# Layer-0 routed experts on one Trainium2 core: the turn of the Gelu products placed behind the next block's gate and up products, down products two steps behind

## The chip, the core and the metric

The kernel runs on one NeuronCore of a Trainium2 chip. The metric is the device time of one execution in microseconds (us). A core has TensorE (PE; its weight loads are PEld in the profile), VectorE (DVE), ScalarE (ACT), GpSimd (POOL) and the queue engine SP; they run their own instruction streams and wait for each other by semaphores.

## What is computed

Two transformer layers over x of 2048 rows of 512 float32. Each is attention, layer norm, mixture of experts, layer norm. The change touches the routed experts of layer 0; cut to that part the reference is

```python
def _experts_all(x, g, gb, w1, b1, w2, b2):       # gelu is the exact one
    y = jax.nn.gelu(jnp.einsum('bsd,edf->bsef', x, g) + gb, approximate=False)
    y = y * (jnp.einsum('bsd,edf->bsef', x, w1) + b1)
    return jnp.einsum('bsef,efd->bsed', y, w2) + b2

aff = jax.nn.sigmoid(jnp.einsum('bsd,de->bse', x, wa))
topk_p, topk_i = jax.lax.top_k(aff, K)            # K = 2 of E = 16 experts
topk_p = topk_p / jnp.sum(topk_p, axis=-1, keepdims=True)
combine = jnp.sum(jax.nn.one_hot(topk_i, E, dtype=x.dtype) * topk_p[..., None], axis=2)
routed = jnp.einsum('bsed,bse->bsd', _experts_all(x, rg, rgb, rw1, rb1, rw2, rb2), combine)
```

with d = 512 and f = 256. Only the two chosen experts of a row are computed by the kernel.

## The kernel before, in words

`two_layers` runs its stages one after the other: `attention0`, `experts0_shared` (which also makes the routing tables), `experts0_routed`, `attention1` (which gathers the experts' results), `experts1_shared`, `experts1_routed`, `combine1`. Between stages all engines meet.

Matmuls in float32 precision are made of three: every operand is split into a high part (a copy to fp32r, made by ScalarE) and a low part (original minus high, made by VectorE), and `mm3` (lines 66 to 68) issues high x high, high x low and low x high.

`experts0_routed` works on NG0 = 47 blocks of 128 gathered rows, numbered g. The routing sorts the rows by expert into groups of 128. Block g = 4h + p takes group 12p + h, so that four columns (p = 0 to 3) walk through the groups side by side; blocks that share p share raw buffers, so raw buffers are four deep. The split tiles (`w1_hi`, `w2_lo`, `xt_hi`, `hf`, ...) and the PSUM banks are two deep (g % 2). For each block:

- GpSimd asks for three indirect DMAs: `rows` (L1043, 256 KB of token rows into `xg`), `gate_up` (L1051, 1 MB of gate and up weights into `w1_raw`) and `down` (L1059, 512 KB of down weights into `w2_raw`). `load_of` holds an index out of bounds where the group before in the column has the same expert; nothing is moved then. Each request for a block waits until the block four earlier has let its buffer go: `rows` for the turn of the tokens, `gate_up` for the low split L1176, `down` for the low split L1193.
- TensorE: `turn` (L1082, four transposes of the tokens), `gate_up` (12 matmuls of 512 columns and the bias L1097), `turn_hidden` (L1104, two transposes of the Gelu products `hf`), `down` (six matmuls of 512 columns).
- ScalarE: `turned_hi` (L1128, high part of the turned tokens), `hidden_hi` (L1142, high part of the turned products), `weights_hi` (L1135, 128 x 2048), the copy of the down weights (L1149, 128 x 1024) and Gelu (L1153), both in `gelu`, and `results` (L1160, the output to `y`, which SP stores).
- VectorE: `turned_lo` (L1180), `hidden_lo` (L1184), `weights_lo` (L1176, 128 x 2048), and in `hidden` the product `hf` = Gelu x up (L1191), followed by the low part of the down weights (L1193, 128 x 1024).

The order is written out by hand. A step g of TensorE is `turn`(g+1), `turn_hidden`(g-1), `gate_up`(g), `down`(g-1). `three_stages` gives a step of ScalarE as turned_hi(g+1), hidden_hi(g-1), weights_hi(g+1), gelu(g), results(g-1), and of VectorE as turned_lo(g+1), hidden_lo(g-1), weights_lo(g+1), hidden(g). TensorE and GpSimd are written out in full; ScalarE and VectorE run a loop of four steps a round.

Of the kernel before, what the change touches and what calls it, by code (L numbers as in the profile page):

```python
# [487 lines left out]
def three_stages(eng, n, first, second, third, ahead=no_work, between=no_work, prepare=no_work, unroll=2, lead=3):  # L488

    def step(g):

        for stage, item in ((ahead, g + lead), (first, g + 1), (between, g - 1), (prepare, g + 1), (second, g), (third, g - 1)):
            if 0 <= item < n:
                stage(item // unroll, item % unroll)


    rounds = (n - lead - 1) // unroll
    for g in range(-lead, unroll + 1):
        step(g)
    with eng.Fori(1, rounds) as i:
        for q in range(unroll):
            at = lambda stage, item: stage(i + item // unroll, item % unroll)
            at(ahead, q + lead + 1)
            at(first, q + 2)
            at(between, q)
            at(prepare, q + 2)  # L510
            at(second, q + 1)
            at(third, q)
    for g in range(unroll * rounds + 1, n + 1):
        step(g)


# [7 lines left out]
NG0 = (2 * T) // GRP + E0 - 1  # L524
# [465 lines left out]
def experts0_routed(k):  # L990
# [3 lines left out]
    U = U0  # L994
    with ExitStack() as ctx:
# [22 lines left out]
        nothing = lambda h, p: None  # L1018
# [3 lines left out]
        with nc.Block() as block:  # L1022
# [52 lines left out]
            @block.tensor  # L1075
            def _(pe):
                def turn(h, p):
                    pe.wait_ge(s_g[p], 16 * (h + 1))
                    if past(h, p, 2):
                        pe.wait_ge(s_tlo, U * h + p - 1)  # L1080
                    for b in range(KD):
                        mm = pe.transpose(bank[p % 2][:, b * P:(b + 1) * P], xg[p][:, b * P:(b + 1) * P], k.ident[:, :])  # L1082
                    mm.then_inc(s_tps, 1)

                def gate_up(h, p):
                    g = U * h + p
                    if not past(h, p, 1):
                        pe.wait_ge(s_b1lo, 1)
                    pe.wait_ge(s_wlo, g + 1)
                    pe.wait_ge(s_tlo, g + 1)  # L1090
                    if past(h, p, 2):
                        pe.wait_ge(s_h, g - 1)
                    out = bank[2 + p % 2][:, :]
                    for b in range(KD):
                        t, c = slice(b * P, (b + 1) * P), slice(b * 2 * F0, (b + 1) * 2 * F0)
                        mm3(pe, out, xt_hi[p][:, t], xt_lo[p][:, t], w1_hi[p][:, c], w1_lo[p][:, c], b == 0, False)
                    pe.matmul(out, k.expert_here[:, NH0 * p + h:NH0 * p + h + 1].to_broadcast([P, P]), b1[:, :], start=False, stop=True).then_inc(s_gu, 1)  # L1097

                def turn_hidden(h, p):
                    pe.wait_ge(s_h, U * h + p + 1)  # L1100
                    if past(h, p, 2):
                        pe.wait_ge(s_hlo, U * h + p - 1)
                    for f in range(FB):
                        mm = pe.transpose(bank[4 + p % 2][:, f * P:(f + 1) * P], hf[p][:, f * P:(f + 1) * P], k.ident[:, :])  # L1104
                    mm.then_inc(s_ht, 1)

                def down(h, p):
                    g = U * h + p
                    pe.wait_ge(s_hlo, g + 1)
                    pe.wait_ge(s_vlo, g + 1)  # L1110
                    if past(h, p, 2):
                        pe.wait_ge(s_ysb, g - 1)
                    for f in range(FB):
                        t, c = slice(f * P, (f + 1) * P), slice(f * D, (f + 1) * D)
                        mm = mm3(pe, bank[6 + p % 2][:, :], ht_hi[p][:, t], ht_lo[p][:, t], w2_hi[p][:, c], w2_lo[p][:, c],
                                 f == 0, f == FB - 1)
                    mm.then_inc(s_dn, 1)

                for g in range(-1, NG0 + 1):
                    for stage, item in ((turn, g + 1), (turn_hidden, g - 1), (gate_up, g), (down, g - 1)):  # L1120
                        if 0 <= item < NG0:
                            stage(item // U, item % U)

            @block.scalar
            def _(act):
                def turned_hi(h, p):
                    act.wait_ge(s_tps, U * h + p + 1)
                    act.activation(xt_hi[p][:, :], bank[p % 2][:, :], ACT.Copy).then_inc(s_thi, 1)  # L1128

                def weights_hi(h, p):  # L1130
                    g = U * h + p
                    act.wait_ge(s_w[p], 16 * (h + 1))
                    if past(h, p, 2):
                        act.wait_ge(s_gu, g - 1)
                    act.activation(w1_hi[p][:, :], w1_raw[p][:, :], ACT.Copy).then_inc(s_whi, 1)  # L1135

                def hidden_hi(h, p):
                    g = U * h + p
                    act.wait_ge(s_ht, g + 1)
                    if past(h, p, 2):  # L1140
                        act.wait_ge(s_dn, g - 1)
                    act.activation(ht_hi[p][:, :], bank[4 + p % 2][:, 0:FB * P], ACT.Copy).then_inc(s_hh, 1)  # L1142

                def gelu(h, p):
                    g = U * h + p
                    act.wait_ge(s_v[p], 16 * (h + 1))
                    if past(h, p, 2):
                        act.wait_ge(s_dn, g - 1)
                    act.activation(w2_hi[p][:, :], w2_raw[p][:, :], ACT.Copy).then_inc(s_vhi, 1)  # L1149
                    act.wait_ge(s_gu, g + 1)  # L1150
                    if past(h, p, 2):
                        act.wait_ge(s_h, g - 1)
                    act.activation(ge[p][:, :], bank[2 + p % 2][:, 0:F0], ACT.Gelu).then_inc(s_ge, 1)  # L1153

                def results(h, p):
                    g = U * h + p
                    act.wait_ge(s_dn, g + 1)
                    if past(h, p, U):
                        act.wait_ge(s_y[p], 16 * h)
                    act.activation(y[p][:, :], bank[6 + p % 2][:, :], ACT.Copy).then_inc(s_ysb, 1)  # L1160

                three_stages(act, NG0, turned_hi, gelu, results, between=hidden_hi, prepare=weights_hi, unroll=U)

            @block.vector
            def _(vec):
                lo_rows = slice(32, 32 + E0)
                vec.wait_ge(s_b1, 32)
                vec.wait_ge(s_zero, 1)
                vec.tensor_copy(b1[0:E0, :], b1_raw[0:E0, :]).then_inc(s_b1hi, 1)
                vec.tensor_copy(b1_hi[lo_rows, :], b1_raw[lo_rows, :]).then_inc(s_b1hi, 1)  # L1170
                vec.wait_ge(s_b1hi, 2)
                vec.tensor_tensor(b1[lo_rows, :], b1_raw[lo_rows, :], b1_hi[lo_rows, :], ALU.subtract).then_inc(s_b1lo, 1)

                def weights_lo(h, p):
                    vec.wait_ge(s_whi, U * h + p + 1)
                    vec.tensor_tensor(w1_lo[p][:, :], w1_raw[p][:, :], w1_hi[p][:, :], ALU.subtract).then_inc(s_wlo, 1)  # L1176

                def turned_lo(h, p):
                    vec.wait_ge(s_thi, U * h + p + 1)
                    vec.tensor_tensor(xt_lo[p][:, :], bank[p % 2][:, :], xt_hi[p][:, :], ALU.subtract).then_inc(s_tlo, 1)  # L1180

                def hidden_lo(h, p):
                    vec.wait_ge(s_hh, U * h + p + 1)
                    vec.tensor_tensor(ht_lo[p][:, :], bank[4 + p % 2][:, 0:FB * P], ht_hi[p][:, :], ALU.subtract).then_inc(s_hlo, 1)  # L1184

                def hidden(h, p):
                    g = U * h + p
                    vec.wait_ge(s_ge, g + 1)
                    if past(h, p, 2):
                        vec.wait_ge(s_ht, g - 1)  # L1190
                    vec.tensor_tensor(hf[p][:, :], ge[p][:, :], bank[2 + p % 2][:, F0:2 * F0], ALU.mult).then_inc(s_h, 1)  # L1191
                    vec.wait_ge(s_vhi, g + 1)
                    vec.tensor_tensor(w2_lo[p][:, :], w2_raw[p][:, :], w2_hi[p][:, :], ALU.subtract).then_inc(s_vlo, 1)  # L1193

                three_stages(vec, NG0, turned_lo, hidden, nothing, between=hidden_lo, prepare=weights_lo, unroll=U)


H1, DH1, FM = 16, 32, 64
# [1495 lines left out]
```

## Time and profile before

| | us |
|---|---|
| median of 3 runs (1604.08 to 1609.27) | 1608.56 |
| the profiled execution, its own time | 1606.87 |
| its span in the trace | 1605.1 |
| first token transpose of the stage | at 428.33 |
| last copy of its results | at 693.10 |

Times in the trace count from the start of the span. A row of the timeline gives start, duration, engine, line, what is written and read, and in brackets how long the engine stood idle before and who ended that. A row of the waits gives who waited for whom, total, number of times and longest. A request on GpSimd is a DMA_INDIRECT; its own duration is the engine's, the transfer lands later.

### The profile page before, as it was taken

To read this page: it belongs to the slowest core of one execution; us is meant where nothing else is said; L and a number is where in the kernel's file an instruction comes from. 1 tells how busy PE (TensorE), PEld (TensorE's weight loads), DVE (VectorE), ACT (ScalarE), POOL (GpSimd) and SP (SyncE) were. 2 spreads that over 40 slices of the span, in tenths; PEclk is the share of its full clock that TensorE was granted. 3 is DMA by queue.
4 is the path that set the end of the run, shared out by engine and by line. 5 is a ranking of instruction groups with operands and counts; after the bars stand their busy time and mean duration, and the time that the engine had idled before them with its cause. 6 is when DMAs were issued, how large, how long until landed. Compare 5 with 4: busy or idle time off the path is not lost. (4 is left out here: it accounts for less than half of the span.)

```text
span 1605.1 us, 21477 instructions
## 1 busy us (share of the span) xinstructions
PE 1358.1 (85%) x7252; PEld 1118.4 (70%) x7253; DVE 1074.1 (67%) x1792; ACT 728.6 (45%) x1157; POOL 750.3 (47%) x656
## 2 busy tenths in 40 slices
PE   6999869999699999925999689996698899999960
PEld 5787647766477777725999688995566777777740
DVE  5688747232388888846885556764393688888857
ACT  4121132000188888822554354441422388888850
POOL 1455510000488887632664324331056467777744
PEclk9899979999799999967999899997799799999995
DMA  4000040000456566533110100000512899999958
GB/s 165 1 1 27 27 132 2 1 0 0 161 190 222 170 208 226 171 120 95 52 53 2 31 3 1 28 27 27 194 40 103 319 335 341 342 346 346 345 134 314
DMA packets 81807, 212.67 MB, mean 132 GB/s; under 512 B 20425, under 2 KB 23497, under 8 KB 79291
## 3 DMA queue, kind: packets, MB, share of 16 engines
q1 hardware_dynamic: 50075, 133.14, 22.7%
q0 software_dynamic: 31120, 77.38, 17.0%
q8 instruction: 51, 0.84, 0.2%
q10 hardware_dynamic: 528, 1.05, 0.2%
q14 instruction: 33, 0.27, 0.1%
HBM read 208.75 MB, written 46.79 MB: 159 GB/s over the span
## 5 line engine op out<-in xcount | busy, mean ns | idle before, releaser
L66 PE MATMUL bank<-e_w_hi,e_xt_hi 128*96 128x384 f32 (+1 forms) x444 | 169.3, 381 | 3.4 <-DVE e_w_lo L2551 3.4
L68 PE MATMUL bank<-e_w_hi,e_xt_lo 128*96 128x384 f32 (+1 forms) x444 | 161.8, 364 | 0.0
L67 PE MATMUL bank<-e_w_lo,e_xt_hi 128*96 128x384 f32 (+1 forms) x444 | 161.3, 363 | 0.0
L1051 POOL DMA_INDIRECT e_w_raw<-in_w_gate_up,r_load_of x47 | 53.4, 1135 | 218.5 <-issue 218.5
L2441 POOL DMA_INDIRECT sums<-e_y,r_target_of x64 | 110.2, 1722 | 70.1 <-DMA sums<-e_y,r_target_of 44.0
L1176 DVE TENSOR_TENSOR e_w_lo<-e_w_raw,e_w_hi 128x2048 fp32r<-128x2048 f32 x47 | 107.7, 2292 | 33.8 <-ACT e_w_hi L1135 33.8
L2551 DVE TENSOR_TENSOR e_w_lo<-r_w_early,e_w_hi 128x1536 fp32r<-128x1536 f32 x48 | 84.9, 1768 | 24.4 <-ACT e_w_hi L2515 24.4
L1043 POOL DMA_INDIRECT e_xg<-rows,r_token_of x47 | 93.2, 1983 | 14.3 <-issue 14.3
L231 POOL TENSOR_TENSOR a_read<-a_read_n 128x256 f32<-128x256 f32 x64 | 50.2, 785 | 103.1 <-DVE a_read_n L452 103.1
L1675 POOL TENSOR_TENSOR q_g_lo<-q_gf,q_g_hi 128x512 fp32r<-128x512 f32 x32 | 41.5, 1298 | 111.9 <-ACT q_g_hi L1789 111.9
L1135 ACT ACTIVATE e_w_hi<-e_w_raw 128x2048 fp32r<-128x2048 f32 x47 | 89.8, 1910 | 0.0
L66 PE MATMUL bank<-e_w_hi,e_ht_hi 128*96 128x512 f32 (+1 forms) x222 | 87.6, 395 | 2.4 <-DVE e_ht_lo L2563 1.2
L67 PE MATMUL bank<-e_w_lo,e_ht_hi 128*96 128x512 f32 (+1 forms) x222 | 87.4, 394 | 0.0
L68 PE MATMUL bank<-e_w_hi,e_ht_lo 128*96 128x512 f32 (+1 forms) x222 | 87.1, 392 | 0.0
L66 PEld LDWEIGHTS bank<-e_w_hi,e_xt_hi 128*96 128x96 f32 (+1 forms) x444 | 77.6, 175 | 12.3 <-DVE e_w_lo L2551 3.6
L68 PEld LDWEIGHTS bank<-e_w_hi,e_xt_lo 128*96 128x96 f32 (+1 forms) x444 | 77.6, 175 | 11.9
L67 PEld LDWEIGHTS bank<-e_w_lo,e_xt_hi 128*96 128x96 f32 (+1 forms) x444 | 78.0, 176 | 8.8
L66 PE MATMUL bank<-s_xt_hi,s_w_hi 128*128 128x512 f32 (+1 forms) x192 | 77.0, 401 | 0.8 <-ACT s_scores L2200 0.8
L68 PE MATMUL bank<-s_xt_hi,s_w_lo 128*128 128x512 f32 (+1 forms) x192 | 76.1, 396 | 0.0
L67 PE MATMUL bank<-s_xt_lo,s_w_hi 128*128 128x512 f32 (+1 forms) x192 | 75.7, 394 | 0.0
L2515 ACT ACTIVATE e_w_hi<-r_w_early 128x1536 fp32r<-128x1536 f32 x48 | 71.3, 1484 | 0.0
L1059 POOL DMA_INDIRECT e_w_raw<-in_w_down,r_load_of x47 | 60.5, 1287 | 17.3 <-issue 16.1
(461 smaller groups left out, 4361.7 us busy)
## 6 DMA issues: line engine op xcount, KB each, us to landing
r_w_early<-in_w_gate_up SPq DMA_DIRECT2D x48, 768.0 KB, 16.6
r_w_early<-in_w_down SPq DMA_DIRECT2D x24, 768.0 KB, 13.2
results<-e_y SPq DMA_DIRECT2D x47, 256.0 KB, 5.0
rows<-resid SPq DMA_DIRECT2D x8, 1024.0 KB, 4.3
r_w_first<-in_w_gate_up SPq DMA_DIRECT2D x8, 768.0 KB, 16.4
e_w_raw<-in_w_down SPq DMA_DIRECT2D x8, 768.0 KB, 13.5
e_w_raw<-in_w_gate_up SPq DMA_DIRECT2D x8, 768.0 KB, 16.1
resid<-in_x SPq DMA_DIRECT2D x4, 1024.0 KB, 12.5
```

What stands on the lines that cost most here:

```text
L66: pe.matmul(out, a_hi, b_hi, start=start, stop=False)
L67: pe.matmul(out, a_hi, b_lo, start=False, stop=False)
L68: return pe.matmul(out, a_lo, b_hi, start=False, stop=stop)
L231: pool.tensor_tensor(read_2[:, v % 2, :], read_n[:, v % 2, 0:256], read_n[:, v % 2, 256:512], ALU.add).then_inc(s_r2, 1)
L1043: pool.indirect_dma_start(xg[p][:, :], None, k.rows, bass.IndirectOffsetOnAxis(k.token_of[:, c:c + 1], 0)).then_inc(s_g[p], 16)
L1051: pool.indirect_dma_start(w1_raw[p][:, :], None, io["w_gate_up0"], bass.IndirectOffsetOnAxis(k.load_of[:, c:c + 1], 0), bounds_check=E0 * ...
L1059: pool.indirect_dma_start(w2_raw[p][:, :], None, io["w_down0"], bass.IndirectOffsetOnAxis(k.load_of[:, c:c + 1], 0), bounds_check=E0 * P - ...
L1135: act.activation(w1_hi[p][:, :], w1_raw[p][:, :], ACT.Copy).then_inc(s_whi, 1)
L1176: vec.tensor_tensor(w1_lo[p][:, :], w1_raw[p][:, :], w1_hi[p][:, :], ALU.subtract).then_inc(s_wlo, 1)
L2441: pool.indirect_dma_start(k.sums[p % 2], bass.IndirectOffsetOnAxis(k.target_of[:, e:e + 1], 0), y[p][:, :], None, compute_op=ALU.add).then ...
L2515: act.activation(w1_hi[p][:, :, :], w1_raw[p][:, :, :], ACT.Copy).then_inc(s_whi, 1)
L2551: vec.tensor_tensor(w1_lo[p][:, :, :], w1_raw[p][:, :, :], w1_hi[p][:, :, :], ALU.subtract).then_inc(s_wlo, 1)
```

## The change

`turn_hidden` moves behind `gate_up` on TensorE, and `down` goes from one step behind to two. ScalarE and VectorE follow: the down weights' two splits leave `gelu` and `hidden`, become `down_hi` and `down_lo`, and stand one step later, behind the parts of the turned products. A new helper `pipeline` takes the stages of an engine with how far each is ahead and issues them in that order. Buffers, GpSimd's queue, SP's stores and every single instruction stay as they are.

```diff
+def pipeline(eng, n, unroll, *stages):
+
+    def step(g):
+        for stage, ahead in stages:
+            if 0 <= g + ahead < n:
+                stage((g + ahead) // unroll, (g + ahead) % unroll)
+
+    first, last = -max(ahead for _, ahead in stages), -min(ahead for _, ahead in stages)
+    rounds = (n + first - 1) // unroll
+    for g in range(first, 2 * unroll + 1):
+        step(g)
+    with eng.Fori(2, rounds) as i:
+        for q in range(unroll):
+            for stage, ahead in stages:
+                stage(i + (q + 1 + ahead) // unroll, (q + 1 + ahead) % unroll)
+    for g in range(unroll * rounds + 1, n + last):
+        step(g)
...
-                for g in range(-1, NG0 + 1):
-                    for stage, item in ((turn, g + 1), (turn_hidden, g - 1), (gate_up, g), (down, g - 1)):
+                for g in range(-1, NG0 + 2):
+                    for stage, item in ((turn, g + 1), (gate_up, g), (turn_hidden, g - 1), (down, g - 2)):
...
-                def gelu(h, p):
+                def down_hi(h, p):
                     g = U * h + p
                     act.wait_ge(s_v[p], 16 * (h + 1))
                     if past(h, p, 2):
                         act.wait_ge(s_dn, g - 1)
                     act.activation(w2_hi[p][:, :], w2_raw[p][:, :], ACT.Copy).then_inc(s_vhi, 1)
+
+                def gelu(h, p):
+                    g = U * h + p
                     act.wait_ge(s_gu, g + 1)
...
-                three_stages(act, NG0, turned_hi, gelu, results, between=hidden_hi, prepare=weights_hi, unroll=U)
+                pipeline(act, NG0, U, (turned_hi, 1), (weights_hi, 1), (gelu, 0), (hidden_hi, -1), (down_hi, -1), (results, -2))
...
-                    vec.wait_ge(s_vhi, g + 1)
+
+                def down_lo(h, p):
+                    vec.wait_ge(s_vhi, U * h + p + 1)
                     vec.tensor_tensor(w2_lo[p][:, :], w2_raw[p][:, :], w2_hi[p][:, :], ALU.subtract).then_inc(s_vlo, 1)
...
-                three_stages(vec, NG0, turned_lo, hidden, nothing, between=hidden_lo, prepare=weights_lo, unroll=U)
+                pipeline(vec, NG0, U, (turned_lo, 1), (weights_lo, 1), (hidden, 0), (hidden_lo, -1), (down_lo, -1))
```

TensorE before, from the bias matmul that ends one block's gate and up to the first matmul of the next block's:

```order
L1097 MATMUL bank<-e_b,r_expert_here 128x512
L66 MATMUL bank<-e_w_hi,e_ht_hi 128x512
L67 MATMUL bank<-e_w_lo,e_ht_hi 128x512
L68 MATMUL bank<-e_w_hi,e_ht_lo 128x512
L66 MATMUL bank<-e_w_hi,e_ht_hi 128x512
L67 MATMUL bank<-e_w_lo,e_ht_hi 128x512
L68 MATMUL bank<-e_w_hi,e_ht_lo 128x512
L1082 MATMUL bank<-ident,e_xg 128x128 x4
L1104 MATMUL bank<-ident,e_hf 128x128 x2
L66 MATMUL bank<-e_w_hi,e_xt_hi 128x512
```

and the same place with the change (L1101 is L1082 before, L1116 is L1097, L1123 is L1104):

```order
L1116 MATMUL bank<-e_b,r_expert_here 128x512
L1123 MATMUL bank<-ident,e_hf 128x128 x2
L66 MATMUL bank<-e_w_hi,e_ht_hi 128x512
L67 MATMUL bank<-e_w_lo,e_ht_hi 128x512
L68 MATMUL bank<-e_w_hi,e_ht_lo 128x512
L66 MATMUL bank<-e_w_hi,e_ht_hi 128x512
L67 MATMUL bank<-e_w_lo,e_ht_hi 128x512
L68 MATMUL bank<-e_w_hi,e_ht_lo 128x512
L1101 MATMUL bank<-ident,e_xg 128x128 x4
L66 MATMUL bank<-e_w_hi,e_xt_hi 128x512
```

The two transposes of the products (L1104, L1123) moved from between the token transposes and gate and up to between gate and up and down.

VectorE before, one step (numbers are the buffers; `w1_raw3` is block 3):

```order
L1180 TENSOR_TENSOR e0_xt_lo1<-bank1,e0_xt_hi1 128x512
L1184 TENSOR_TENSOR e0_ht_lo1<-bank5,e0_ht_hi1 128x256
L1176 TENSOR_TENSOR e0_w1_lo1<-e0_w1_raw3,e0_w1_hi1 128x2048
L1191 TENSOR_TENSOR e0_hf0<-e0_ge0,bank2 128x256
L1193 TENSOR_TENSOR e0_w2_lo0<-e0_w2_raw2,e0_w2_hi0 128x1024
```

and with the change (L1202 is L1180 before, L1198 is L1176, L1213 is L1191, L1206 is L1184, L1217 is L1193):

```order
L1202 TENSOR_TENSOR e0_xt_lo1<-bank1,e0_xt_hi1 128x512
L1198 TENSOR_TENSOR e0_w1_lo1<-e0_w1_raw3,e0_w1_hi1 128x2048
L1213 TENSOR_TENSOR e0_hf0<-e0_ge0,bank2 128x256
L1206 TENSOR_TENSOR e0_ht_lo1<-bank5,e0_ht_hi1 128x256
L1217 TENSOR_TENSOR e0_w2_lo1<-e0_w2_raw1,e0_w2_hi1 128x1024
```

The low part of the turned products moved from ahead of the gate and up split to behind the product, and the down split in a step is that of block 1 where it was that of block 2.

## Rows read from the trace of the kernel before

**Rows 1.** The page: span, and part 1, busy time of each engine

```profile
span 1605.1 us, 21477 instructions
...
PE 1358.1 (85%) x7252; PEld 1118.4 (70%) x7253; DVE 1074.1 (67%) x1792; ACT 728.6 (45%) x1157; POOL 750.3 (47%) x656
```

**Rows 2.** Timeline, VectorE: gate and up split of blocks 2 and 46

```profile
445.23 2.29 DVE L1176 TENSOR_TENSOR e_w_lo<-e_w_raw,e_w_hi 128x2048 fp32r<-128x2048 f32 x1 [0.69 <-ACT e_w_hi L1135]
...
682.49 2.29 DVE L1176 TENSOR_TENSOR e_w_lo<-e_w_raw,e_w_hi 128x2048 fp32r<-128x2048 f32 x1 [0.69 <-ACT e_w_hi L1135]
```

**Rows 3.** Waits, 440 to 700 us: total, times, longest

```profile
DVE e_w_lo L1176 <- ACT e_w_hi L1135: 32.7, 46, 1.1
...
PEld bank L1104 <- DVE e_hf L1191: 18.4, 46, 1.0
```

**Rows 4.** Timeline, 565.8 to 571.5 us, one step on TensorE, ScalarE and VectorE

```profile
565.86 0.60 PE L1082 MATMUL bank<-ident,e_xg 128*128 128x128 f32 x4
...
566.11 0.41 DVE L1191 TENSOR_TENSOR e_hf<-e_ge,bank 128x256 f32<-128x256 f32 x1
566.44 1.22 DVE L1193 TENSOR_TENSOR e_w_lo<-e_w_raw,e_w_hi 128x1024 fp32r<-128x1024 f32 x1
566.55 0.59 ACT L1128 ACTIVATE e_xt_hi<-bank 128x512 fp32r<-128x512 f32 x1
566.58 0.44 PE L1104 MATMUL bank<-ident,e_hf 128*128 128x128 f32 x2
...
566.77 0.47 PE L66 MATMUL bank<-e_w_hi,e_xt_hi 128*128 128x512 f32 x1
...
567.05 0.39 ACT L1142 ACTIVATE e_ht_hi<-bank 128x256 fp32r<-128x256 f32 x1
...
567.33 1.91 ACT L1135 ACTIVATE e_w_hi<-e_w_raw 128x2048 fp32r<-128x2048 f32 x1
...
569.27 2.29 DVE L1176 TENSOR_TENSOR e_w_lo<-e_w_raw,e_w_hi 128x2048 fp32r<-128x2048 f32 x1 [0.69 <-ACT e_w_hi L1135]
...
569.60 0.40 PE L1097 MATMUL bank<-e_b,r_expert_here 128*128 128x512 f32 x1
...
571.21 0.60 PE L1082 MATMUL bank<-ident,e_xg 128*128 128x128 f32 x4
...
571.49 0.41 DVE L1191 TENSOR_TENSOR e_hf<-e_ge,bank 128x256 f32<-128x256 f32 x1
```

**Rows 5.** Timeline, the same step on GpSimd, its three requests

```profile
567.33 1.19 POOL L1051 DMA_INDIRECT e_w_raw<-in_w_gate_up,r_load_of  x1 [0.31 <-issue]
568.83 0.99 POOL L1059 DMA_INDIRECT e_w_raw<-in_w_down,r_load_of  x1 [0.30 <-issue]
570.12 2.29 POOL L1043 DMA_INDIRECT e_xg<-rows,r_token_of  x1 [0.30 <-issue]
```

**Rows 6.** Timeline, 431 to 436 us, GpSimd and VectorE while the stage fills

```profile
431.75 0.96 POOL L1043 DMA_INDIRECT e_xg<-rows,r_token_of  x1 [0.30 <-issue]
431.91 2.29 DVE L1176 TENSOR_TENSOR e_w_lo<-e_w_raw,e_w_hi 128x2048 fp32r<-128x2048 f32 x1 [1.11 <-ACT e_w_hi L1135]
433.02 2.04 POOL L1059 DMA_INDIRECT e_w_raw<-in_w_down,r_load_of  x1 [0.31 <-issue]
```

**Rows 7.** DMA issues, us to landing: 460 to 500 us; 497 to 498.5 us

```profile
e_w_raw<-in_w_gate_up,r_load_of POOLq DMA_INDIRECT x8, 3.4
...
e_xg<-rows,r_token_of POOLq DMA_INDIRECT x8, 5.4
...
e_w_raw<-in_w_gate_up,r_load_of POOLq DMA_INDIRECT x1, 7.6
```

**Rows 8.** Timeline, 441 to 443 us: token transposes and their copy, ScalarE free

```profile
441.44 0.60 PE L1082 MATMUL bank<-ident,e_xg 128*128 128x128 f32 x4
...
442.08 0.60 ACT L1128 ACTIVATE e_xt_hi<-bank 128x512 fp32r<-128x512 f32 x1
```

## The prediction

> **What bounds the kernel now.** The page comes first: the profiled execution spans 1605.1 us, TensorE is its busiest engine [rows 1]. The change touches only layer 0's routed experts: 47 blocks of 128 rows, some 260 us. I count in steps, one block a step. From the split of block 2's gate and up weights to that of block 46 there are 44 steps in 682.49 - 445.23 = 237.26 us, **5.39 us a step** [rows 2].
>
> The waits of the stage come next [rows 3]. TensorE's weight loads stood before the turn of the Gelu products (L1104) 46 times, 18.4 us in all: 0.40 us a step, what the change aims at. Just as steady is VectorE's wait for ScalarE before L1176, 32.7 us.
>
> One step in order of time says why [rows 4]. Take T = 565.86, the first transpose of the next block's tokens. The product `hf` begins at T+0.25, because VectorE was at L1176; the turn L1104 follows at 566.58, ScalarE copies it out at 567.05, and only then takes the next block's weights (567.33). L1176 waits for that until 569.27, and the next product comes 2.22 us later (the gap between the products of two steps is again 5.38). So the step is a ring: product, turn (0.47), copy (0.47), weight copy (0.28), L1176 (1.94), product (2.22), 5.38 in sum. TensorE waits since the ring is longer than its own work: its matmuls follow at 0.230 us (seven in 571.21 - 569.60 = 1.61).
>
> The last view is GpSimd's queue, which asks for every load of the stage [rows 5, 6]. Undisturbed, a request takes 0.96 us [rows 6], and the next begins 0.30 later. Requests that meet a VectorE instruction with two SBUF inputs end 0.85 us after that instruction. In rows 6 the one from 433.02 meets L1176, which ends at 434.20, and ends itself at 435.06. In rows 5 the one from 567.33 meets the down split L1193 (ends 567.66) and ends at 568.52; the one from 570.12 meets L1176 (ends 571.56) and ends at 572.41. One that begins 0.16 us before L1176 goes through (431.75, 0.96 us). So a request needs something at about 0.13 us after its start that VectorE holds, then 0.85 more. Per step GpSimd makes three requests: one is released by L1176's end, one by the down split's end, and the third needs a gap of 0.85 + 0.30 + 0.13 = 1.28 us after the latter, before L1176 begins again.
>
> **The change part by part.** No instruction is added or removed. What moves:
>
> 1. TensorE: the turn of the products goes behind gate and up, down products to the next step. The ring is broken. Without waits TensorE needs 19 x 0.230 = 4.37, six transposes at about 0.11 (0.19 to 0.23 for two, from 566.58 to the next matmul, estimated 0.64 in all) = 5.01, and one loop jump of ScalarE and VectorE in four steps, about 0.02 to 0.05 a step: **5.06**. Bounds: 4.99, if the whole 0.40 [rows 3] goes, and 5.11, if only the 0.28 between four transposes' 0.44 and the 0.72 from 565.86 to 566.58 goes. Gain alone: 0.33 x 44 = 14.5 us.
>
> 2. ScalarE: weight copy right behind the token copy, at T+0.69+0.49 = T+1.18 rather than T+1.47. VectorE's L1176 then runs from T+3.12 to T+5.41. Gate and up of that block are to begin at T+5.06+0.44 = T+5.50: 0.1 in hand, so this costs nothing, but a later load shows at once.
>
> 3. VectorE: the order is now L1176, product, low part of the turned products (0.33), **down split**. The down split ends 2.22+0.33+0.33+1.22 = 4.10 us after L1176's start; before, 2.22+0.33+1.22 = 3.77. That changes GpSimd's sum. It gets its third request in a step only if the step is at least 3.77+1.28 = 5.05 before (it was 5.39) and 4.10+1.28 = **5.38** after. A 5.06 step is too short by 0.32: GpSimd then makes two requests of three and falls behind, until TensorE waits for loads.
>
> 4. The down request of a block waits for the down split four blocks earlier, which comes a step later. The row request and the gate-and-up request of the next block are queued behind it. Their lead shrinks: before, the gate-and-up request at T+1.47 was ten us ahead of its use (two steps), the row request likewise, so landing times of 5.4 and 7.6 us [rows 7] were hidden.
>
> 5. What is late next. Once GpSimd is behind, a block's row request is released by the down split's end; the rows land about 3.9 us after release (5.4 from start less the 1.44 us held: rows 5, 7); turn, token copy and weight copy take 0.64 [rows 8] +0.49+1.94 = 3.07 to the next L1176. This loop spans two steps: (4.10+3.9+3.07)/2 = **5.53 us a step** where no new weights are loaded, 0.14 worse than before.
>
> 6. Steps with new weights. `load_of` skips a load when the block before in its column has the same expert. The reference's own routing of its inputs gives 19 real loads in 47 blocks, 15 of them behind the first four: 5, 6, 13, 14, 16, 21, 22, 26, 30, 32, 33, 36, 37, 41, 42. A skipped load is through in 3.4 us, a real one takes 7.6 [rows 7]. In the loop of point 5 the gate-and-up request begins 1.15 after the rows' release and its copy on ScalarE is due at 3.9+1.13 = 5.03, so 3.9 us later: a skipped load just fits, a real one is 3.7 late. Some 0.5 of it is in hand before gate and up. The step is then 8.3 or so, 2.9 over before.
>
> I carried these terms block by block through the stage as a recurrence (each instruction starts when its engine is free and its inputs are there). With the old order it gives 5.39 a step and row landings of 5.4, 7.1 and 8.2 us, which is a check. With the new order: seven steps with a first load +2.9 each = 20.3; two where GpSimd had caught up, +0.9 = 1.8; six second loads in a row +1.1 = 6.6 (rows queue behind 1.5 MB of weights); nine steps behind a load -0.28 = -2.5, since a stall lets GpSimd catch up; the 20 plain ones +0.14 = 2.8. Sum **+29**. Filling is 2.3 shorter (no down products in the first step), draining 2.1 longer (one more step with the last down split before it); together nothing. Later stages start later by the same amount. 1606.87 + 29 = **1636 us**. The profiled execution lies 0.1% under the median of 1608.56, within the spread of its three runs.
>
> The Trainium skill (SBUF — State Buffer, Who interferes with whom) says that a VectorE tensor_tensor never has a two-port mode and did not stall a GpSimd-issued DMA in its probe, with only GpSimd's reads held by two SBUF inputs. The rows above show such requests held, 2.04 and 2.29 us against 0.96; these are indirect ones, so reading the index could be what is held. By the probe's outcome points 3 and 5 would fall away.
>
> **The rivals.**
> - *Faster: GpSimd keeps its lead.* If requests can slip into the gaps or a request's need comes earlier than 0.13, no load is late and only point 1 stays: 1606.87 - 14 = 1593. It decides at a step of 5.38; for it speaks that before the change no TensorE wait for a load is left once the stage runs. Against it: 0.32 us missing is twice what rows 6 leave open. 0.14.
> - *VectorE does not hold requests at all* (rows 5 and 6 would be chance). Then only point 4 is left: real loads 1 to 2 us late, -14 + 15 x 1 to 1.5 = between -6 and +9: 1607. Chance 0.07.
> - *Only the pace is lost, loads stay hidden.* Stalls give back enough lead: 44 x 0.14 = +6, 1613. Chance 0.12.
> - *Worse:* a request slips a slot in every plain step, the loop is (4.10+1.28+3.9+3.07)/2 = 6.18, or the TensorE clock drops to its lower level in the stalls: 44 x 0.79 = 35 plus a third of the loads' sum, some 1655. Chance 0.07.
> - The forecast: 0.60.
>
> **How the numbers follow.** A measurement tells about 0.3% (4.8 us) from no change. Faster: 0.14 and a bit of the second rival, 0.16. Same: most of the second and a little of the third, 0.09. Slower: 0.75. The recurrence moves between +22 and +43 when landing and load times are varied within the rows. The range of 1606 to 1652 leaves out the fast case and half of the worst.
>
> **What the profile after would show.** Right: weight-load waits for the products (L1104, now L1123) gone; new waits of TensorE on `e_xg`'s DMA in plain steps and of ScalarE on `e_w_raw`'s DMA in blocks 5, 13, 16, 21; GpSimd requests of over 2 us twice a step instead of once; steps of 5.5 and 8 us side by side; some 29 us more in the stage. Wrong: an even step near 5.06 with no DMA release before TensorE, or request durations that don't end 0.85 us after a VectorE split.

## The result and the profile after

| | us | before on the same chips | ratio |
|---|---|---|---|
| changed kernel, median of 4 runs | 1643.17 (1636.09 to 1646.78) | 1606.38 (1604.08 to 1609.27) | 1.0227 (1.0204 to 1.025) |
| predicted | 1636.0 (1606 to 1652) | 1608.56 | |
| profiled execution | 1636.09 | 1606.87 | |

It is slower, by 37 us at the medians. The profiled execution was the fastest of the four; the three without a profile took 1640.74 to 1646.78. So the trace below accounts for some 30 us, and another 5 to 11 us of the other runs have no trace of their own.

The page of the changed kernel, with the span and part 1, answers to [rows 1]:

```profile
span 1634.4 us, 21478 instructions
...
PE 1366.7 (84%) x7253; PEld 1123.9 (69%) x7253; DVE 1074.5 (66%) x1792; ACT 732.9 (45%) x1157; POOL 764.5 (47%) x656
```

No engine was given more work, but GpSimd, which only asks for transfers in this stage, is busy 14.2 us longer, and TensorE 8.6 us. Of the latter 7.6 lie in the stage: the same 1175 matmuls take 257.98 rather than 250.37 us, at a granted clock of 0.95 on average rather than 0.98. The timeline of the changed kernel, with the first token transpose and the last copy of results of the stage (start, duration, engine, instruction, idle before it and what ended it):

```profile
425.58 1.11 PE L1101 MATMUL bank<-ident,e_xg 128*128 128x128 f32 x4 [8.44 <-DMA e_xg<-rows,r_token_of]
...
720.19 0.60 ACT L1182 ACTIVATE e_y<-bank 128x512 f32<-128x512 f32 x1 [1.22 <-PE bank L68]
```

The stage takes 294.6 us; between the same two instructions of before it was 693.10 - 428.33 = 264.8. Filling and draining are nearly even (29.8 in the stage, 44 x 0.66 = 29.1 in the steps). All of the difference of the two spans (29.3) is in this stage (29.8). The splits of blocks 2 and 46, VectorE's timeline of the changed kernel, answer to [rows 2]:

```profile
441.77 2.29 DVE L1198 TENSOR_TENSOR e_w_lo<-e_w_raw,e_w_hi 128x2048 fp32r<-128x2048 f32 x1 [1.11 <-ACT e_w_hi L1154]
...
708.10 2.29 DVE L1198 TENSOR_TENSOR e_w_lo<-e_w_raw,e_w_hi 128x2048 fp32r<-128x2048 f32 x1 [2.26 <-ACT e_w_hi L1154]
```

44 steps in 266.33 us, **6.05 us a step** instead of 5.39. The waits of the changed kernel, 430 to 730 us (total, times, longest), answer to [rows 3]:

```profile
DVE e_w_lo L1198 <- ACT e_w_hi L1154: 60.3, 43, 5.8
PEld bank L1101 <- DMA e_xg<-rows,r_token_of: 36.9, 26, 6.8
...
ACT e_w_hi L1154 <- DMA e_w_raw<-in_w_gate_up,r_load_of: 31.6, 16, 5.1
...
POOL e_w_raw L1078 <- DVE e_w_lo L1217: 25.5, 10, 6.8
...
PEld bank L66 <- DVE e_w_lo L1198: 12.4, 15, 2.2
```

The wait that the change aims at (the turn of the products, now L1123, on `e_hf`) is not in the list any more; it was 18.4 us. In its place stand two waits for transfers: the tokens' transposes for the gathered rows, 26 times, and ScalarE for the gate and up weights, 16 times. VectorE's 60.3 is the same lateness seen one engine on, and is not to be added.

Why transfers are late is read from VectorE and GpSimd side by side. Timeline of the changed kernel, 476 to 488 us, blocks without a real load:

```profile
476.65 2.29 DVE L1198 TENSOR_TENSOR e_w_lo<-e_w_raw,e_w_hi 128x2048 fp32r<-128x2048 f32 x1 [0.87 <-ACT e_w_hi L1154]
...
477.61 2.20 POOL L1078 DMA_INDIRECT e_w_raw<-in_w_down,r_load_of  x1 [0.30 <-issue]
...
479.53 1.22 DVE L1217 TENSOR_TENSOR e_w_lo<-e_w_raw,e_w_hi 128x1024 fp32r<-128x1024 f32 x1
...
480.11 1.47 POOL L1062 DMA_INDIRECT e_xg<-rows,r_token_of  x1 [0.30 <-issue]
...
481.88 0.99 POOL L1070 DMA_INDIRECT e_w_raw<-in_w_gate_up,r_load_of  x1 [0.30 <-issue]
...
487.63 2.29 DVE L1198 TENSOR_TENSOR e_w_lo<-e_w_raw,e_w_hi 128x2048 fp32r<-128x2048 f32 x1 [0.41 <-ACT e_w_hi L1154]
...
487.76 3.02 POOL L1070 DMA_INDIRECT e_w_raw<-in_w_gate_up,r_load_of  x1 [0.30 <-issue]
```

The down request ends at 479.81, 0.87 after L1198's end (478.94); the row request at 481.58, 0.83 after the down split's end (480.75). The third finds the gap and takes 0.99. That is the forecast's picture, with two held requests a step. The last pair is a missed slot: the request begins 0.13 us after L1198 and is held for all of it, 3.02 us; in [rows 6] one that began 0.16 before L1176 went through. The fence also shows what does not happen: L1198 takes 2.29 us whether or not a request meets it.

A step behind a real load (block 13), same view, 507 to 510 us:

```profile
507.05 1.91 ACT L1154 ACTIVATE e_w_hi<-e_w_raw 128x2048 fp32r<-128x2048 f32 x1 [3.23 <-DMA e_w_raw<-in_w_gate_up,r_load_of]
...
509.00 2.29 DVE L1198 TENSOR_TENSOR e_w_lo<-e_w_raw,e_w_hi 128x2048 fp32r<-128x2048 f32 x1 [3.43 <-ACT e_w_hi L1154]
...
509.61 0.66 PE L1101 MATMUL bank<-ident,e_xg 128*128 128x128 f32 x4 [1.53 <-DMA e_xg<-rows,r_token_of]
```

ScalarE waits 3.23 us for the weights, VectorE 3.43 for ScalarE; this step takes 8.13 us.

The durations of all 47 row requests (lowest/median/highest in ns, first to last us, by line), the changed kernel first, then before:

```profile
L1062 POOL DMA_INDIRECT e_xg<-rows,r_token_of x47: 960/1466/2982, 420.7 to 699.5; - x47
```

```profile
L1043 POOL DMA_INDIRECT e_xg<-rows,r_token_of x47: 962/2286/2737, 423.3 to 669.8; - x47
```

Before, the row request alone paid for L1176 in most steps, and the step had room for it. After, row, gate-and-up and down requests take turns in paying, and some pay 3.0 us. Of the 141 requests of all three kinds, 80 take over 1.2 us instead of 47.

### The profile page after: what moved, and what is told of

Its sections match the earlier page's. It is cut to its first block and busy times, and to the rows that moved or that the text cites. A ratio compares the mean times of both kernels' runs of the same rounds, so it can differ in the third digit from the quotient of the medians.

```text
span 1634.4 us, 21478 instructions
## 1 busy us (share of the span) xinstructions
PE 1366.7 (84%) x7253; PEld 1123.9 (69%) x7253; DVE 1074.5 (66%) x1792; ACT 732.9 (45%) x1157; POOL 764.5 (47%) x656
## 5 line engine op out<-in xcount | busy, mean ns | idle before, releaser
L66 PE MATMUL bank<-e_w_hi,e_xt_hi 128*96 128x384 f32 (+1 forms) x444 | 172.6, 389 | 12.2 <-DVE e_w_lo L1198 8.7
L1070 POOL DMA_INDIRECT e_w_raw<-in_w_gate_up,r_load_of x47 | 69.4, 1476 | 215.6 <-issue 215.6
L1198 DVE TENSOR_TENSOR e_w_lo<-e_w_raw,e_w_hi 128x2048 fp32r<-128x2048 f32 x47 | 107.8, 2293 | 60.3 <-ACT e_w_hi L1154 60.3
L1078 POOL DMA_INDIRECT e_w_raw<-in_w_down,r_load_of x47 | 81.9, 1743 | 37.5 <-DVE e_w_lo L1217 25.5
L66 PE MATMUL bank<-e_w_hi,e_ht_hi 128*96 128x512 f32 (+1 forms) x222 | 91.9, 414 | 2.6 <-issue 1.4
L1062 POOL DMA_INDIRECT e_xg<-rows,r_token_of x47 | 69.4, 1476 | 14.3 <-issue 14.3
```

What stands on the lines that cost most here:

```text
L66: pe.matmul(out, a_hi, b_hi, start=start, stop=False)
L1062: pool.indirect_dma_start(xg[p][:, :], None, k.rows, bass.IndirectOffsetOnAxis(k.token_of[:, c:c + 1], 0)).then_inc(s_g[p], 16)
L1070: pool.indirect_dma_start(w1_raw[p][:, :], None, io["w_gate_up0"], bass.IndirectOffsetOnAxis(k.load_of[:, c:c + 1], 0), bounds_check=E0 * ...
L1078: pool.indirect_dma_start(w2_raw[p][:, :], None, io["w_down0"], bass.IndirectOffsetOnAxis(k.load_of[:, c:c + 1], 0), bounds_check=E0 * P - ...
```

## The experiments

Theory A is the forecast's: two-input VectorE instructions hold GpSimd's requests, the down split now stands too late for three requests a step (point 3), and a down request waiting for its buffer keeps the next rows and weights behind it (point 4). Its rivals: holding is harmless and only the queue order counts; only real loads are late and the pace does not matter; the new order itself costs TensorE time. (The letters B to F in the recorded expectations stand for what each of them says beside its letter.) "Stage" below is from the first token transpose to the last copy of results.

| kernel | us | before | ratio (interval) | stage us | us a step |
|---|---|---|---|---|---|
| before | 1606.38 | | | 264.8 | 5.39 |
| after | 1643.17 | 1606.38 | 1.0227 (1.0204 to 1.025) | 294.6 | 6.05 |
| e1 no real loads | 1624.18 | 1605.0 | 1.0113 (1.0095 to 1.013) | 283.7 | 5.82 |
| e2 before, no real loads | 1605.29 | 1605.0 | 1.000 (0.9989 to 1.001) | 263.9 | 5.39 |
| e3 one SBUF input | 1607.99 | 1605.0 | 1.0019 (1.0 to 1.0038) | 267.8 | 5.46 |
| e4 one input, no real loads | 1597.13 | 1605.0 | 0.9942 (0.9925 to 0.9958) | 255.8 | 5.18 |
| e5 down request later | 1622.9 | 1604.23 | 1.0118 (1.0096 to 1.0141) | 282.6 | 5.79 |
| e6 one input, request later | 1599.06 | 1604.23 | 0.9973 (0.9963 to 0.9983) | 259.6 | 5.23 |
| e7 down split earlier | 1626.51 | 1604.25 | 1.0139 (1.0108 to 1.017) | 287.1 | 5.90 |
| e8 halved split, request later | 1587.95 | 1604.23 | 0.9889 (0.9868 to 0.9909) | 247.9 | 5.01 |
| e9 before, one SBUF input | 1606.21 | 1604.25 | 1.001 (0.9995 to 1.0024) | 266.2 | 5.45 |
| e10 as e7, no real loads | 1591.8 | 1604.23 | 0.9927 (0.9903 to 0.9952) | 254.2 | 5.13 |
| e11 halved split alone | 1619.16 | 1604.25 | 1.0103 (1.0064 to 1.0142) | 273.8 | 5.61 |
| e12 down split earlier, request later | 1592.87 | 1604.25 | 0.9911 (0.9884 to 0.9939) | 252.2 | 5.10 |

**Real loads: e1 on the changed kernel, e2 on before.** Every block from the second in its column on counts as having the same expert as the one before it, so only the first weights are loaded; the requests stay, but bring nothing.

```diff
-step(vec.tensor_tensor(same[:, 1:NG0], gef[:, 1:NG0], gef[:, 0:NG0 - 1], ALU.is_equal))
+step(vec.memset(same[:, 1:NG0], 1.0))
```

> The changed order with every weight load after the first of each column skipped by its index (the outputs are not the reference's; the requests stay). Theory A (GpSimd's requests held by VectorE's two-input splits, three requests a step fit only from 5.38 us on): plain steps of 5.5 us, TensorE still waits for e_xg, stage about 270 us against 265 before, 1612 us. Rival B (only the real loads are late, nothing else): steps of 5.06, 1593 us. Rival C (TensorE's new order itself costs): hardly below the changed kernel, 1640 us.

> The order of before with the same loads skipped (outputs not the reference's). Control: loads were hidden before, so steps of 5.39 and 1606 us as before by every theory; anything faster would say that the loads cost something before too.

e2 came out as expected: before hides all of its real loads. e1 keeps most of the loss: 10.9 us of the stage go, 18.9 stay. So it is not true that only real loads are late: the plain pace alone costs more than half. It also missed my size, 5.82 us a step against 5.5. The waits of e1, 430 to 720 us, show the kind, and its timeline the reason:

```profile
PEld bank L1101 <- DMA e_xg<-rows,r_token_of: 47.7, 38, 6.6
```

```profile
517.92 2.29 DVE L1198 TENSOR_TENSOR e_w_lo<-e_w_raw,e_w_hi 128x2048 fp32r<-128x2048 f32 x1 [0.48 <-ACT e_w_hi L1154]
...
517.98 3.10 POOL L1070 DMA_INDIRECT e_w_raw<-in_w_gate_up,r_load_of  x1 [0.30 <-issue]
...
524.79 2.29 DVE L1198 TENSOR_TENSOR e_w_lo<-e_w_raw,e_w_hi 128x2048 fp32r<-128x2048 f32 x1 [2.18 <-ACT e_w_hi L1154]
```

The gate-and-up request begins 0.06 us after the split, misses its slot and is held to 521.08; the next split then comes 6.87 us after the last. 19 of e1's steps took 6.0 us or more. A GpSimd that is behind does not settle into an even, slightly longer step; it slips, a slot at a time.

**The hold: e3 on the changed kernel, e9 on before.** The second input of both weight splits is read from PSUM, one broadcast column (in e9 the down split's column is in the other bank of the pair). The instruction's length stays, and so does every wait.

```diff
-vec.tensor_tensor(w1_lo[p][:, :], w1_raw[p][:, :], w1_hi[p][:, :], ALU.subtract).then_inc(s_wlo, 1)
+vec.tensor_tensor(w1_lo[p][:, :], w1_raw[p][:, :], bank[p % 2][:, 0:1].to_broadcast([P, KD * 2 * F0]), ALU.subtract).then_inc(s_wlo, 1)
...
-vec.tensor_tensor(w2_lo[p][:, :], w2_raw[p][:, :], w2_hi[p][:, :], ALU.subtract).then_inc(s_vlo, 1)
+vec.tensor_tensor(w2_lo[p][:, :], w2_raw[p][:, :], bank[p % 2][:, 0:1].to_broadcast([P, FB * D]), ALU.subtract).then_inc(s_vlo, 1)
```

> The changed order, with the second input of the two weight splits taken from a PSUM column that is spread over the row instead of from the high part in SBUF (low parts of the weights are then wrong): the same lengths of instruction, one SBUF input each. Theory A: requests all 0.96 to 0.99 us, plain steps 5.06 to 5.1; real loads still late by 1 to 3 us because the down request waits a step longer and the next block's stand behind it: stage 268 to 275, 1611 to 1617 us. Rival D (the hold is chance or comes from DMA traffic): requests stay at 2 us and more, time stays at 1640.

> Control: the order of before with the one-input form of the two splits (low parts of the weights wrong). By every theory the ring of product, turn, copy, weight copy and split stays, steps of 5.39, 1605 us; GpSimd's requests fall to 0.97 us each. Anything faster would say that the one-input form itself speeds VectorE up.

Requests and splits of e3, all 47 of each, by line (lowest/median/highest ns):

```profile
L1062 POOL DMA_INDIRECT e_xg<-rows,r_token_of x47: 963/967/985, 421.1 to 672.0; - x47
```

```profile
L1198 DVE TENSOR_TENSOR e_w_lo<-e_w_raw,bank x47: 2279/2287/2291, 429.6 to 681.7; 128x2048 fp32r<-128x2048 f32 x47
```

No request is held, though VectorE works as long as ever; the stage loses 26.8 of its 29.8 us. So holding is not harmless. At 267.8 us and 1607.99 e3 is a little faster than the 268 to 275 us and 1611 to 1617 expected. In before the same edit gives nothing (e9), as the step had room for the hold (5.37, every fourth 5.45; its mean has one step of 8.04 in it). The waits of e3, 430 to 720 us, show what is left:

```profile
POOL e_w_raw L1078 <- DVE e_w_lo L1217: 78.2, 37, 8.1
...
ACT e_w_hi L1154 <- DMA e_w_raw<-in_w_gate_up,r_load_of: 15.6, 13, 2.7
```

GpSimd, now quick, stands before the down request for its buffer 37 times, and real loads are still late 13 times: point 4 by itself.

**Both: e4.** The edits of e3 and e1.

> Both of the above: one SBUF input in the splits and no loads after the first of each column (outputs not the reference's). Theory A: nothing is late, point 1 alone is left, steps 5.06, stage 250 us, 1592 us. Rival C (the new order itself costs): above 1606 us.

From block 5 on the steps take 5.0 to 5.25 us, all but the one of 9.22 and its neighbours: here the ring is broken and nothing holds it, which measures point 1 at about 0.29 us a step, 12.8 in all. It also excludes that the new order itself costs. The odd step, 9.22, follows a stop of GpSimd that no wait explains (last section). The median, 1597.13, lies 5 us above the 1592 expected, about the size of that step's excess.

**Queue order: e5.** The down request of a block goes behind the rows and the gate and up weights of the second block after it, so that its wait holds nothing up.

```diff
                     rows(g // U, g % U)
                     gate_up(g // U, g % U)
-                    down(g // U, g % U)
+                    if g > U + 1:
+                        down((g - 2) // U, (g - 2) % U)
+                for g in range(NG0 - 2, NG0):
+                    down(g // U, g % U)
```

> The changed order, with each block's down request on GpSimd placed behind the row and gate-and-up requests of the block two later, so that its longer wait holds up nothing that is due earlier. Theory A: the wait is gone, but three requests a step still don't fit under 5.38 us, so most of the loss stays: stage 282 to 290 us against 295 for the changed kernel, 1628 to 1635 us. Rival E (the queue behind the down request is the whole cause): everything hidden, stage 250, 1593 us.

12.0 us of the stage come back, and at 1622.9 us the kernel is 5 us faster than the lower end of what was expected; it is far from the 1593 of a queue order that would be the whole cause. GpSimd's three requests in e5, 440 to 700 us (busy us, mean ns; idle before them and its releaser):

```profile
L1070 POOL DMA_INDIRECT e_w_raw<-in_w_gate_up,r_load_of x42 | 78.6, 1870 | 12.8 <-issue 12.8
L1078 POOL DMA_INDIRECT e_w_raw<-in_w_down,r_load_of x43 | 71.4, 1660 | 13.1 <-issue 13.1
L1062 POOL DMA_INDIRECT e_xg<-rows,r_token_of x42 | 67.8, 1613 | 12.8 <-issue 12.8
```

Nothing waits for a buffer; busy and issue time make 78.6 + 71.4 + 67.8 + 38.7 = 256.5 of 260 us. GpSimd's queue is full with requests alone, and is the bound of the stage. From block 5 to block 10 the steps took 5.04 to 5.13 us, and then, the lead spent, those of blocks 11 to 15 took 6.3 to 8.7; steps of both kinds follow.

**Both causes off: e6.** The edits of e3 and e5.

> The same, and the two weight splits with one SBUF input (low parts of the weights wrong). Theory A: neither the hold nor the wait is left, real loads are hidden again, steps of 5.06 to 5.1 throughout, stage 250 us (up to 5 more if GpSimd stops once for several us as it did in the last runs), 1592 us. Rival F (real loads are late for want of DMA bandwidth at the shorter step): steps above 6 us remain at the blocks with real loads, 1600 us and more.

Steps of 4.95 to 5.25 from block 5 to block 36, with real loads too, so the DMA bandwidth is enough at this pace; then again one stop of GpSimd (3.69 us) and two long steps (9.38 and 6.96), which is more than the 5 us allowed for: 1599.06 us, where 1592 was expected. The stage is 35.0 us shorter than after's.

**The down split earlier: e7, and e10 without real loads.** On VectorE the down split goes ahead of the low part of the turned products. It needs 0.33 us less behind L1198, so the threshold of point 3 is back at 5.05.

```diff
-pipeline(vec, NG0, U, (turned_lo, 1), (weights_lo, 1), (hidden, 0), (hidden_lo, -1), (down_lo, -1))
+pipeline(vec, NG0, U, (turned_lo, 1), (weights_lo, 1), (hidden, 0), (down_lo, -1), (hidden_lo, -1))
```

> Nothing left out. The changed order with the down split on VectorE directly behind the product (as e10), all loads real. Theory A: GpSimd's pace fits (5.05), so plain steps are 5.1; real loads are late as in e3_after_oneinput, because the down request still waits a step longer: stage 268 to 280 us, 1608 to 1620 us, that is at best level with before. Rival: the pace was the whole loss, 1592 us as without loads.

> The changed order without the loads (as e1_after_noload, outputs not the reference's), with the down split on VectorE directly behind the product and ahead of the products' low part. The down split then ends 3.77 us after the gate and up split's start instead of 4.10, so a third request fits from 5.05 us on instead of 5.38. Theory A: steps fall from 5.82 to 5.3 to 5.4, stage 262 to 266 us, 1603 to 1606 us. Rival C: no change against e1_after_noload, 1624 us.

Without real loads the 0.33 us decide it: 5.13 us a step instead of e1's 5.82, better than I had expected. A cut of 0.33 us in the place of one VectorE instruction takes 29.5 us off the stage. With real loads most of it goes again: most of e7's plain steps are 5.0 to 5.2, but seven of the nine steps with a first load take 7.6 to 8.6, and so do two plain ones (blocks 7 and 28). The total lies 6.5 us above the top of what I had expected. Its waits, 430 to 720 us:

```profile
POOL e_w_raw L1078 <- DVE e_w_lo L1217: 41.6, 14, 5.5
ACT e_ge L1175 <- PE bank L1116: 35.9, 32, 4.1
...
ACT e_w_hi L1154 <- DMA e_w_raw<-in_w_gate_up,r_load_of: 25.7, 12, 3.3
```

A quicker GpSimd only reaches the waiting down request sooner. The lead of what stands behind it is fixed by the queue's order, not by its pace.

**A version that keeps both: e12.** The edits of e7 and e5; nothing of the computation is left out.

> Nothing left out. e7 and the down requests placed behind the next two blocks' (as e5). Theory A: pace and lead are both there: steps of 5.1, real loads mostly hidden, stage 254 to 270 us, 1594 to 1610 us; the pace has only 0.01 to 0.05 us to spare, so a slot missed at a late load may cost a few steps of 6 us. Rival: as e5, 1622 us.

1592.87 us, 0.9911 of before (0.9884 to 0.9939), 1 us below the range expected. e5 and e12 differ in the place of the down split alone, and in neither does a steady wait for a buffer hold GpSimd. So the 30.4 us between their stages are what the gap is worth, and not an earlier release of the down buffer. GpSimd and VectorE in e12, 542 to 548 us:

```profile
542.29 1.17 POOL L1078 DMA_INDIRECT e_w_raw<-in_w_down,r_load_of  x1 [0.30 <-issue]
543.76 0.96 POOL L1062 DMA_INDIRECT e_xg<-rows,r_token_of  x1 [0.30 <-issue]
...
543.94 2.29 DVE L1201 TENSOR_TENSOR e_w_lo<-e_w_raw,e_w_hi 128x2048 fp32r<-128x2048 f32 x1 [0.42 <-issue]
...
545.03 2.08 POOL L1070 DMA_INDIRECT e_w_raw<-in_w_gate_up,r_load_of  x1 [0.31 <-issue]
```

The row request begins 0.18 us ahead of the split and slips through: three requests in a step of 5.10, with some 0.2 us to spare (the edge is measured in the last section).

**A wider gap: e8, and e11 without the later request.** Gate and up weights are split in two halves, each in an instruction of its own on ScalarE and VectorE, with the tokens' copies between them. No single instruction then holds a request for more than 1.2 us and what follows it.

```diff
-vec.tensor_tensor(w1_lo[p][:, :], w1_raw[p][:, :], w1_hi[p][:, :], ALU.subtract).then_inc(s_wlo, 1)
+vec.tensor_tensor(w1_lo[p][:, 0:KD * F0], w1_raw[p][:, 0:KD * F0], w1_hi[p][:, 0:KD * F0], ALU.subtract).then_inc(s_wlo, 1)
+def weights_lo_b(h, p):
+    vec.tensor_tensor(w1_lo[p][:, KD * F0:], w1_raw[p][:, KD * F0:], w1_hi[p][:, KD * F0:], ALU.subtract).then_inc(s_wlo, 1)
...
-pipeline(vec, NG0, U, (turned_lo, 1), (weights_lo, 1), (hidden, 0), (hidden_lo, -1), (down_lo, -1))
+pipeline(vec, NG0, U, (weights_lo, 1), (turned_lo, 1), (weights_lo_b, 1), (hidden, 0), (hidden_lo, -1), (down_lo, -1))
...
-pipeline(act, NG0, U, (turned_hi, 1), (weights_hi, 1), (gelu, 0), (hidden_hi, -1), (down_hi, -1), (results, -2))
+pipeline(act, NG0, U, (weights_hi, 1), (turned_hi, 1), (weights_hi_b, 1), (gelu, 0), (hidden_hi, -1), (down_hi, -1), (results, -2))
```

> Nothing left out. The changed order with the down requests placed as above; ScalarE and VectorE split the gate and up weights in two halves, the halves on VectorE with the tokens' low part between them. Theory A: each of the three splits of a step (1.22 us each, ends at least 1.28 us apart) releases one request at its end, so three requests fit into every step; steps of 5.02 to 5.1, stage 247 to 255 us, 1589 to 1597 us, faster than before. Rival: the extra 0.1 us on each engine or the halves' order costs more than it frees, or a held request isn't released in the short gaps: 1606 us or more.

> Nothing left out. e8 without the moved down requests: halves alone. Theory A: pace is there, lead is not, so real loads are late: stage 270 to 289 us, 1610 to 1629 us, against 248 and 1588 for e8. Rival: the halves alone do it, 1588 us.

e11 fell in what was expected, and e8 1 us below it. e8 is the fastest kernel of this study, 1587.95 us, 0.9889 of before (0.9868 to 0.9909), with all steps from block 5 on between 4.94 and 5.11. GpSimd and VectorE in e8, 523 to 528 us, and its wait for weights, 430 to 720 us:

```profile
523.19 1.23 DVE L1204 TENSOR_TENSOR e_w_lo<-e_w_raw,e_w_hi 128x1024 fp32r<-128x1024 f32 x1 [0.29 <-ACT e_w_hi L1157]
...
524.04 1.24 POOL L1070 DMA_INDIRECT e_w_raw<-in_w_gate_up,r_load_of  x1 [0.30 <-issue]
...
524.93 1.22 DVE L1208 TENSOR_TENSOR e_w_lo<-e_w_raw,e_w_hi 128x1024 fp32r<-128x1024 f32 x1
...
525.59 1.43 POOL L1078 DMA_INDIRECT e_w_raw<-in_w_down,r_load_of  x1 [0.31 <-issue]
...
527.32 1.47 POOL L1062 DMA_INDIRECT e_xg<-rows,r_token_of  x1 [0.30 <-issue]
```

```profile
ACT e_w_hi L1157 <- DMA e_w_raw<-in_w_gate_up,r_load_of: 3.3, 1, 3.3
```

Each request meets an instruction, but only for 1.24 to 1.47 us: 1.24 + 1.43 + 1.47 + 0.91 = 5.05 us for three. One wait for weights is left of 16. Halves without the later request (e11) win 20.8 of after's stage, but stay slower than before: the two causes have to go together here as well.

## Why the prediction was right, and where its size was off

The forecast was 1636 and the time 1643.17, in the range. That the profiled execution took 1636.09 is luck: it was the fastest of four, and the slowdown at the medians is 37 us where 29 was forecast. The step lengths of the changed kernel, block by block against 5.39, give its sum by its own terms:

| term | forecast | measured |
|---|---|---|
| nine first loads | +22.1 | +21.2 |
| six second loads | +6.6 | +6.1 |
| nine steps behind a load | -2.5 | -0.3 |
| twenty plain steps | +2.8 | +2.1 |
| sum | +29.0 | +29.1 |

- **Point 1** (ring broken, 5.06 us) holds, but is 12.8 rather than 14.5 us: the clean steps are 5.10 (e12) to 5.01 (e8), 5.03 to 5.18 in e4. It shows only where GpSimd keeps up.
- **Point 3** is what decides. The hold is real (e3), harmless before (e9), and 0.33 us in its place make the difference between 5.82 and 5.13 us a step (e1, e10). Its threshold was too high. It put the moment at which a request can be held 0.13 us after the request's start; the runs show that requests begun up to 0.04 us behind the split's start still go through (last section). The gap needed is then 0.85 + 0.30 - 0.04 = 1.11 us and the threshold 4.10 + 1.11 = 5.21 rather than 5.38. A step of 5.06 misses it by 0.15 us, not by 0.32, and the 5.10 measured by 0.11: the margin was narrower than the forecast had it.
- **Point 4** is real and separate: 12.0 us alone (e5). With the pace repaired it is worth more, 287.1 - 252.2 = 34.9 (e7, e12), and without the hold 267.8 - 259.6 = 8.2 (e3, e6; e6 has a stop of 3.69 us in it).
- **Point 5 is the mis-sized step.** "5.53 us a step where no new weights are loaded" took the loop as even. By itself it is 5.82 (e1), since requests miss slots and pay up to 3.1 us; 19 of e1's steps lie at 6.0 or above, towards the 6.18 of the *Worse* rival. In the full kernel the error hardly shows: plain steps came out at 5.50 on average. I put that down to the stalls behind real loads, which bring GpSimd back into its gaps; no run shows it apart. The terms therefore do not add as I wrote them. Taking the loads away wins 10.9 us, not the 26.2 that their terms came to. So the close agreement of the sum is in part luck: a plain pace taken 0.29 us a step too quick, 12.8 us in all, against loads priced too high.
- **Point 6** holds in kind and size: a first load's step is 7.8 us on average (forecast 8.3 for seven and 6.3 for two), with one of 10.53 and three of 5.6 to 6.9 about it. A part of it may be the clock (below), which the sum left out.
- **Second loads** came where they were expected, at 6.4 on average (5.2 to 8.3).
- **The signs** came, all but one: requests of over 2 us are not twice a step but 36 in all, against 44 before. What grew is the number between 1.2 and 2 us, 44 instead of 3.

Of the rivals, *GpSimd keeps its lead* is what e12 and e8 make of the change, 1592.87 and 1587.95 where it said 1593. One of its two conditions came true, a need earlier than 0.13 us, and was not enough. *VectorE does not hold requests* is e3, 1607.99, where it said 1607; it is excluded as an account of the changed kernel. (The lower end of its sum, -6, does not follow from its terms: -14 + 15 x 1 is +1.) The outcome of the probe (the Trainium skill, SBUF — State Buffer, Who interferes with whom), a tensor_tensor that did not stall a GpSimd-issued DMA, does not carry over to these indirect requests: the trace's 2.0 to 3.1 us stand against 963 to 985 ns with one SBUF input, so two SBUF inputs of a tensor_tensor do hold them. With the rule of the same section that two SBUF inputs contend with GpSimd's reads the trace agrees, as far as these requests read SBUF. Whether it is the read of the index that is held wasn't tried.

What stays open is why three runs of the changed kernel took 5 to 11 us more than the profiled one. That a queue which misses slots is sensitive to small shifts would be a reason, but the spreads don't bear it out: e1, which slips throughout, spreads by 3.7 us, and e3, in which nothing is held, by 12.2. The granted TensorE clock (full is 2.4 GHz) was 0.96 on average over the stage, 440 to 706 us, against 1.00 in before, 440 to 685. It fell to 1.2 GHz in five stretches, some 20 us in all, about the blocks with real loads 13, 21, 33, 36 and 41; over the same blocks it stayed at 2.4 GHz in e1, e8 and e12. Each fall came within 2.2 us of a wait of TensorE of 1.4 to 3.5 us for gathered rows; e1 had such waits of up to 1.9 us without a fall. What that cost wasn't measured apart. The stage's 1175 matmuls took 258.0 us against 250.4 in before and 249.6 in e1, both at 0.98, so some 8 us at most of what is put down to real loads above can be the clock's.

## What to carry to other kernels

When a change moves an instruction on one engine, look at what else that instruction's place sets: here a wait of 0.40 us a step on TensorE was removed, and the down split landed 0.33 us later, in the gap through which GpSimd made its third request. Count an issuing engine's requests as a budget of the step (0.96 to 0.99 us and 0.30 each, plus what holds them), and ask before shortening a step whether the budget still fits. In an in-order queue a request that waits for a buffer sets the lead of all requests behind it, so put those that wait longest last; a faster queue does not help them.

## What was not expected of the hardware

- A request held by VectorE's two-input split ends 0.83 to 0.88 us after it, whatever its start, and a split that holds a request is not longer for it (2281 to 2295 ns; with one SBUF input 2278 to 2291).
- The edge is sharp, and lies behind the split's start. In the eight traces with two-input splits of 2.29 us, every request that began from 0.3 us ahead to 0.043 us behind the split's start took 0.96 to 0.99, and every one from 0.044 on was held (3.11 us for the first). Where one that begins with the split or just behind it goes through, the split is 0.03 to 0.07 us longer instead. Timeline of e1, one such pair (0.04 us):

```profile
496.30 2.37 DVE L1198 TENSOR_TENSOR e_w_lo<-e_w_raw,e_w_hi 128x2048 fp32r<-128x2048 f32 x1 [0.50 <-ACT e_w_hi L1154]
496.33 0.99 POOL L1070 DMA_INDIRECT e_w_raw<-in_w_gate_up,r_load_of  x1 [0.30 <-issue]
```

- In most runs GpSimd stopped once with nothing in the trace that it waited for. Timelines of e4, then e6:

```profile
616.55 1.00 POOL L1078 DMA_INDIRECT e_w_raw<-in_w_down,r_load_of  x1 [4.05 <-issue]
```

```profile
613.18 1.00 POOL L1070 DMA_INDIRECT e_w_raw<-in_w_gate_up,r_load_of  x1 [3.69 <-issue]
```

It stands at the same place in every trace that has it, ahead of the 114th DMA that GpSimd asks for. It is 3.7 to 4.6 us where the splits have one SBUF input (e3, e4, e6, e9), 2.5 in before (at 624.99, hidden under its lead), e2, e7, e10 and e11, 1.2 in after and 0.7 in e8; e1, e5 and e12 have none. A lead shorter than the stop turns it into a step of 8.0 to 9.4 us (e9, e4, e6). What it is wasn't tried.
